# Second stage: projections and softplus sum in front of the skip product, output projection late, gate product between fourth drive and scan

## What is computed

```python
def _mamba(x, in_w, conv_w, conv_b, xproj_w, dt_w, dt_b, A_log, Dvec, out_w):
    xi, z = jnp.split(jnp.einsum('bld,ed->ble', x, in_w), 2, axis=-1)
    xc = silu(causal_conv4(xi) + conv_b)
    dt, Bm, Cm = jnp.split(jnp.einsum('ble,fe->blf', xc, xproj_w), [4, 20], axis=-1)
    dt = softplus(jnp.einsum('blr,er->ble', dt, dt_w) + dt_b)
    # for each of 16 states s, along the sequence:
    #   h = exp(dt * A) * h + dt * B_t * x_t ;  y_t = sum_s h * C_t
    y = (ys + xc * Dvec) * silu(z)
    return jnp.einsum('ble,de->bld', y, out_w)
```

## Time and profile before

| | |
|---|---|
| median of 3 runs | 3953.78 us (3950.43 to 3957.21) |
| the profiled execution | 3949.65 us, its span 3947.8 us |
| PE busy | 3654.2 us, 93% |
| DVE busy | 3749.1 us, 95% |
| ACT busy | 2937.3 us, 74% |
| POOL busy | 3277.5 us, 83% |
| scans (L1601) | 1024, 2297.9 us, 2274 ns each |
| drives by DVE (L1588) | 768, 906.5 us, 1210 ns each |
| reads by POOL (L1537) | 1024, 2398.9 us, 2360 ns each |
| state sums (L1306) | 4096 matmuls, 1921.9 us, 602 ns each |
| read from memory | 1144 MB, 299 GB/s over the span |

### The profile page before, as it was taken

The page is one execution under the profiler, slowest core; times in us unless marked ns, Lnnn a source line. Parts: engine busy times, 40 slices in busy tenths (PEclk is TensorE's granted clock), DMA queues, the critical chain, the costliest instruction groups (busy, mean ns, idle before and its releaser), DMA issues. The chain is left out here.

```text
span 3947.8 us, 34409 instructions
## 1 busy us (share of the span) xinstructions
PE 3654.2 (93%) x8780; PEld 1519.6 (38%) x8780; DVE 3749.1 (95%) x3409; ACT 2937.3 (74%) x4422; POOL 3277.5 (83%) x1542
## 2 busy tenths in 40 slices
PE   7999999899999999999999999999999999999998
PEld 3444444333333333333333333333333333333333
DVE  7778787999999999999999999999999999999998
ACT  3454554787888878888888888878888888878785
POOL 2221222899999999999999999999999999999998
PEclk9999999999999999999999999999999999999999
DMA  4142324888888888898888888888899888988886
GB/s 113 33 130 58 109 74 149 325 344 338 347 348 348 344 345 340 345 350 353 347 342 350 347 347 342 352 347 341 343 353 349 339 346 347 350 340 344 336 348 264
DMA packets 203157, 1181.06 MB, mean 299 GB/s; under 512 B 30960, under 2 KB 31760, under 8 KB 68816
## 3 DMA queue, kind: packets, MB, share of 16 engines
q1 hardware_dynamic: 200128, 1177.64, 77.5%
q10 hardware_dynamic: 2832, 1.23, 0.1%
HBM read 1144.03 MB, written 34.73 MB: 299 GB/s over the span
## 5 line engine op out<-in xcount | busy, mean ns | idle before, releaser
L1537 POOL TENSOR_TENSOR read<-state,bc_all 128x1024 f32<-128x1024 f32 x1024 | 2398.9, 2360 | 117.0 <-DVE state L1601 88.0
L1601 DVE TENSOR_TENSOR_SCAN state<-decays,p_drive 128x1024 f32<-128x1024 f32 x1024 | 2297.9, 2274 | 33.0 <-ACT p_drive L1436 9.8
L1306 PE MATMUL p_y<-read,ident 128*128 128x512 f32 x4096 | 1921.9, 602 | 14.0 <-POOL read L1537 13.9
L1428 ACT ACTIVATE decays<-dt,wa 128x496 f32<-128x496 f32 x2048 | 1337.2, 703 | 121.1 <-DVE state L1601 118.5
L1306 PEld LDWEIGHTS p_y<-read,ident 128*128 128x128 f32 x4096 | 764.9, 191 | 990.6 <-issue 833.2
L1588 DVE TENSOR_TENSOR p_drive<-bc_all,p_dtx 128x1024 f32<-128x1024 f32 x768 | 906.5, 1210 | 0.0
L1554 POOL TENSOR_TENSOR pool_drive<-dtx,bc_all 128x1024 f32<-128x1024 f32 x256 | 602.4, 2353 | 12.2 <-DMA bc_all<-bc_scratch 11.9
L766 POOL TENSOR_TENSOR pad<-map_all,xc 128x512 f32<-128x512 f32 x96 | 138.9, 1476 | 519.1 <-DMA map_all<-map_scratch 498.3
L1436 ACT COPY p_drive<-pool_drive 128x1024 f32<-128x1024 f32 x256 | 260.8, 1019 | 270.8 <-DVE state L1601 270.8
L1302 PE MATMUL p_y<-xconv,d_diag 128*128 128x512 f32 x256 | 144.6, 647 | 202.0 <-DVE gated L1611 202.0
L556 PE MATMUL p_conv<-pad,wm 128*128 128x512 f32 x576 | 267.5, 600 | 1.8 <-issue 1.8
(11 more groups left out here) (162 smaller groups left out, 3214.1 us busy)
## 6 DMA issues: line engine op xcount, KB each, us to landing
bc_all<-bc_scratch SPq DMA_DIRECT2D x1024, 1024.0 KB, 7.3
map_all<-map_scratch SPq DMA_DIRECT2D x48, 512.0 KB, 5.7
norm_rows<-xn SPq DMA_DIRECT2D x32, 280.0 KB, 5.8
norm_in<-norm_rows SPq DMA_DIRECT2D x64, 140.0 KB, 6.6
norm_in<-norm_rows SPq DMA_DIRECT2D x64, 139.8 KB, 7.6
fresh<-in_x SPq DMA_DIRECT2D x32, 256.0 KB, 6.8
x<-in_x SPq DMA_DIRECT2D x32, 256.0 KB, 3.6
mid_x<-x SPq DMA_DIRECT2D x32, 256.0 KB, 6.5
```

The costliest lines, as they stand in the source:

```text
L1306: nc.tensor.matmul(p_y[:], ident[:], read[:, s % DEEP, :], start=False, stop=(s == N - 1)).then_inc(y_added, 1)
L1428: nc.scalar.activation(decays[:, s % DEEP, :].rearrange("p (q t) -> p q t", t=SIDE)[:, :, 1:], dt[b][:, :, 1:], ACT.Exp, scale=wa[m][:, s: ...
L1537: nc.gpsimd.tensor_tensor(read[:, s % DEEP:s % DEEP + 2, :], state[:, s % DEEP:s % DEEP + 2, :], bc_all[s // CHUNK][:, :, 1, :], ALU.mult) ...
L1601: nc.vector.tensor_tensor_scan(state[:, at:at + 2, :].rearrange("p s n -> p (s n)"), decays[:, at:at + 2, :].rearrange("p s n -> p (s n)") ...
```

## The change

It moves work inside the slot of the second stage and adds none. On PE, the softplus sum of u + 1 and both input projections of u + 2 go in front of the skip product at s = 5; B, C and raw dt go from 12 to 10; the output projection of u - 1 goes from 7 to 13. On ACT the copy of dt goes from step 1 to 6, silus from 11 to 8, the copy of B and C and the softplus steps from 13 to 11, the copy out from 8 to 14. On POOL dtx goes from step 5 to 7. On DVE the gate product goes from behind scan 1 to between drive 3 and scan 3. Units 2 and UNITS - 4 keep the output projection early (`AT_OUT_FIRST`), since the next projection needs `cols_in` filled from it. Waits on `left` and `rows_copied` follow the new order. SP's list is not changed.

```diff
-    AT = dict(project_out=7, leave=8, hold_rows=1,
-              project_in=9, project_z=10, silus=11, project_bc=12, project_dt=12, copy_rows=13, soft=13,
-              sum_dt=0, copy_dt=1, dtx=5, copy_dtx=15)
+    AT = dict(hold_rows=1, project_in=5, sum_dt=5, copy_dt=6, dtx=7, silus=8, project_bc=10, copy_rows=11, soft=11,
+              project_out=13, leave=14, copy_dtx=15)
+    AT_OUT_FIRST = dict(AT, project_out=6, leave=7, project_in=8, project_bc=10)
+    OUT_FIRST = (2, UNITS - 4)
...
-        ge(pe, left, u - 2)
+        ge(pe, left, u - 2 if u - 2 in OUT_FIRST else u - 3)
...
         def project_out(u, b, unit, rows_used):
+            ge(pe, left, u)
             pe.wait_ge(rows_copied, rows_used)
...
         def slot(u, b, before, unit, after, later):
+            when = at(u)
             for s in range(N):
+                if s == when["sum_dt"] and after:
+                    sum_dt(pe, u + 1)
+                if s == when["project_in"] and s == LAG and later:
+                    project_conv(pe, u + 2, later)
+                    project_z(pe, u + 2, later)
                 if s == LAG:
                     add_skip(u, b, unit)
...
-                if s == AT["project_out"] and before:
-                    project_out(u - 1, 1 - b, before, u + 2 if after else UNITS)
+                if s == when["project_out"] and before:
+                    rows = u + 2 if u in OUT_FIRST else u + 3
+                    project_out(u - 1, 1 - b, before, min(rows, UNITS))
-                if s == AT["project_in"] and later:
+                if s == when["project_in"] and s > LAG and later:
...
-                if s == AT["sum_dt"] and after:
-                    sum_dt(pe, u + 1)
...
-                if s == AT["leave"] + 1 and u in (2, UNITS - 4):
+                if s == at(u)["leave"] + 1 and u in OUT_FIRST:
...
-                if s == (AT["copy_dt"] if u else 4) and after:
+                if s == AT["copy_dt"] and after:
...
+                scan_pair(u, p + 2)
+                make_drives(u, p + 3)
                 if half == 0 and before:
                     apply_gate(u - 1, 1 - b, before)
-                scan_pair(u, p + 2)
-                make_drives(u, p + 3)
                 scan_pair(u, p + 3)
```

More of the change, by code:

```diff
@@ L1040, in stage2, with at @@
     MOVE_LEAD = 2
-    AT = dict(project_out=7, leave=8, hold_rows=1,
-              project_in=9, project_z=10, silus=11, project_bc=12, project_dt=12, copy_rows=13, soft=13,
-              sum_dt=0, copy_dt=1, dtx=5, copy_dtx=15)
+    AT = dict(hold_rows=1, project_in=5, sum_dt=5, copy_dt=6, dtx=7, silus=8, project_bc=10, copy_rows=11, soft=11,
+              project_out=13, leave=14, copy_dtx=15)
+    AT_OUT_FIRST = dict(AT, project_out=6, leave=7, project_in=8, project_bc=10)
+    OUT_FIRST = (2, UNITS - 4)
+    def at(u):
+        return AT_OUT_FIRST if u in OUT_FIRST else AT
     def sb(name, shape, dt=f32):
@@ L1343, in slot @@
                     project_conv(pe, u + 2, later)
-                if s == AT["project_z"] and later:
                     project_z(pe, u + 2, later)
-                if s == AT["project_bc"] and later:
+                if s == when["project_bc"] and later:
                     project_bc(pe, u + 2, b, later)
-                if s == AT["project_dt"] and later:
                     project_dt(pe, u + 2, b, later)
-                if s == AT["sum_dt"] and after:
-                    sum_dt(pe, u + 1)
         pe.wait_ge(s1["gn_v"], 16)
@@ L1504, in slot @@
                     hold_rows(u - 2, u)
-                if s == AT["leave"] + 1 and u in (2, UNITS - 4):
+                if s == at(u)["leave"] + 1 and u in OUT_FIRST:
                     hold_rows(u - 1, None if u == 2 else u + 1)
-                if s == AT["leave"] and before:
+                if s == at(u)["leave"] and before:
                     if before[0] == ROWS:
```

## The result

The changed kernel takes 4002.35 us (median of 4 runs, 3996.54 to 4005.18) against 3954.91 us for the kernel before on the same chip: a ratio of 1.0121, 95% interval 1.0109 to 1.0134. The change makes the kernel 1.2% slower. The profiled execution's span is 4001.6 us, 53.8 more than before.

What follows compares the result with a forecast made beforehand. VectorE was taken as the bound. From the profiled 3949.65 us: -21.3 (gate's place), -9.8 (old clock falls), +8.8 (two exceptional units), +56.1 (new falls) = 3983 us; the forecast's own range 3960 to 4008, with rival 1 3922 to 4008.

Steps and rivals of the forecast that it cites:

- What bounds the kernel: Second stage: VectorE, busy 990 of 1000 us, sets the clock; one unit takes 25.19 us.
- the gate's 0.17 us: VectorE: the gate product between drive 3 and scan 3 saves 0.17 us a unit, 21.3 us over 125 units.
- Rival 4: VectorE: the drain rule holds and the gate's new place gives nothing, 4004 us; chance 0.03.
- The chain of 18.35 to 18.46 against 18.38: Pair 2's scan to next scan 0: the chain over TensorE and ScalarE equals VectorE's own way within 0.1 us; nothing charged.
- The hole moves and becomes 1.99 and 1.55 us: TensorE's idle wait moves from skip to z: 1.99 us in rows units, 1.55 in cols.
- The falls of the clock: TensorE behind waits before z: 34 drops to 1.2 GHz at 1.65 us each, +56.1 us (bounds 23 and 110).
- the wait's length decides: TensorE: seven clock falls followed some thirty waits of 1.90 us, none those of 1.85; so 1.99 brings more.
- After a fall the next fall is likelier: TensorE: a fall lengthens its next wait by 0.6 us, to 2.6 in rows units and 2.1 in cols.
- The clock rule: TensorE: a skill page warns only of longer idle gaps; by it no wait of this size would cost anything.
- my first rival: TensorE before z: no or few clock falls, so 3927 us, faster; chance 0.25.
- The two exceptional units and the opening: Units 2 and UNITS - 4: 4.4 us each, +8.8, bounds 0 and 6 each; opening and end nothing, +-3.
- the seven old falls: Steady stage of the kernel before: seven clock falls after 1.90 us waits, which the change removes, -9.8 us.

Runs made afterwards that it cites:

- e7: e4 with the gate product back behind scan 1: 3942.39 us, ratio 0.9971 to the kernel before.
- e4: The changed kernel with ScalarE's copy of dt in step 5 instead of 6: 3929.64 us, ratio 0.9939 to the kernel before.
- e6: e2 with the conv of every unit, rows and cols, issued twice to fill the waits: 4005.41 us, ratio 1.0132 to the kernel before.
- e1: The changed kernel with the conv projection of rows units issued twice, filling the wait before z: 3951.37 us, ratio 0.9994 to the kernel before.
- e2: The changed kernel with the gate product back behind scan 1: 4206.76 us, ratio 1.0640 to the kernel before.
- e5: The changed kernel with only the first product of a rows unit's conv issued twice, half e1's filling: 3960.67 us, ratio 1.0022 to the kernel before.
- e3: The kernel before with the gate product alone moved between drive 3 and scan 3: 4630.70 us, ratio 1.1711.
- e10: e4 with the gate product behind scan 1 in units 2 and UNITS - 4 alone: 3917.66 us, ratio 0.9911 to the kernel before.
- e9: e5 with the z product of rows units fed from 128 partitions instead of 64: 3936.61 us, ratio 0.9960 to the kernel before.
- e11: The changed kernel with only the z product of rows units fed from 128 partitions: 3968.60 us, ratio 1.0039 to the kernel before.

## Why the prediction was right, and where it was off

I forecast 3983 us, slower, with 3960 to 4008 as the forecast's own range; 4002 lies near its upper end.

- **What bounds the kernel** and the gate's 0.17 us: right. The undisturbed unit is 25.00 us against 25.02; e7 against e4 gives 0.19 by itself. The page rule of the Trainium skill that I weighed ("VectorE: DVE Perf Modes", "The DRAIN you can't avoid") does not hold for a scan behind its own drive: 0.19 us a unit are there when the scan follows at once and gone with the gate product between. Rival 4, which followed that rule, had 4004 us, nearer to the measured 4002 than my 3983, but for the wrong reason.
- **The chain of 18.35 to 18.46 against 18.38**: right in size. Undisturbed rows units are 25.04 and, the second, 25.21, so the chain is longer than VectorE's way by 0.04 to 0.2 in them, where I had said within 0.1. I charged nothing; over the middle 115 units it costs 8.7 us. e6 measured the chain itself: 25.5 to 25.8 us a unit, against 25.6.
- **The hole moves and becomes 1.99 and 1.55 us**: measured 1.95 in most first rows units, 1.5 to 1.6 in cols, and 2.16 in most second rows units, where I had made no difference. In 13 of the 30 first ones it is only 0.8 to 1.8; where it is 1.2 or less, TensorE had waited longer for reads of GpSimd before. Of the 0.21, ScalarE's step from the drive copy to the copy of dt is 0.08 (2386.08 to 2387.12 is 1.04, against 0.96 in the earlier trace rows); the rest I did not trace.
- **The falls of the clock**: the mechanism was right, shown by e1 (fill the wait, and 51 us are back) and e6 against e2. I took 34 falls in 62 rows units at 1.65. In the middle there are 27, and against the undisturbed unit of their kind they cost 22 times 1.70 and five times 3.35, together 54.0, so 2.0 each. The single fall of 1.65 was right; that one kind costs twice as much I had not seen. In the five the clock was low from z on and for longer, as at 1033.80, where z, skip and six state sums took 10.60 us against the 7.3 of the prediction's terms:

```profile
1033.80 1.80 PE L1257 MATMUL p_b<-norm_in,wi_rows 64*128 64x512 f32 x2 [1.95 <-ACT dt L1404]
1035.52 2.07 PE L1304 MATMUL p_y<-xconv,d_diag 128*128 128x512 f32 x2
1037.39 7.08 PE L1308 MATMUL p_y<-read,ident 128*128 128x512 f32 x12
```

  The product of the two, 56.1 against 54.0, was right partly by luck: fewer falls, and dearer ones. My step "the wait's length decides" failed, in the changed kernel by falls behind 1.61 to 1.69 us and by 23 against 6 in second and first rows units, and again in e5 (falls behind 1.3 us) and e6 (none behind 1.5). What else decides, and why the second rows unit is so much worse, is open. "After a fall the next fall is likelier" did not show: behind a fall come mostly cols units, whose wait stays at 1.59, and after the five large ones the second rows unit waited 2.63 without one. e2 doesn't show it either.
- **The clock rule** (my first rival, by the "HAM oscillation" section of the page "TensorE: Matmul & The Clock Gate" of the Trainium skill): waits of 1.3 to 2.2 us, shorter than its gaps, bring falls; the runs decide against it here. The rival's 3927 us, though, is not what this order takes without falls: less 54.0 us in the middle and 1.7 each in units 4 and 121, the profiled 4003.4 us would be some 3946 (an estimate), as the chain and the ends cost what both had left out. e4's 3930 has another place for the copy of dt.
- **The two exceptional units and the opening**: the step that was most mis-sized. I gave 4.4 us to each and nothing to opening and end. Units 2 and 124 cost 6.0 and 5.9 more than before, at my bound of 6, the units behind them 1.3 each, and units 0 and 1 cost 4.2 and 2.5. In unit 2 TensorE waits 4.29 us for the later gate product and then works at the low clock; the copy of the output ends 11.4 us behind the start of pair 2's scan, where I had 8.8, and VectorE waits 5.9 us for the decays behind it (5.1 in unit 124). In unit 0 it waits 1.4 and 3.0 us for decays, in unit 1 2.6 us for the copy of drive 0; TensorE waits 4.9 and 3.7 us before z in these two, with the clock low at z. Opening and end together cost 23.6 instead of 8.8, two falls of 1.7 (units 4 and 121) among them. These 14.8 us and the chain's 8.7 are more than the 20 us between 3983 and the profiled 4003.4; a little less for the falls (2.1), the gate (0.6), the seven old falls (0.2) and the start (0.6) makes up the rest.

## What to carry to other kernels

Where an engine off the bound is given a new order, look for the place to which its idle time moves, and for what it meets there: here one wait of about 2 us cost more than waits of 1 us and less in another place, since TensorE's clock fell behind it. Work out the chain that ends in the bound's next instruction, and keep some cover in it; here a copy placed one step sooner (e4) gave that cover and turned the sign of the whole change. Move a consumer later on the bound only together with the work that fills its producer's wait (e3, e10).

## What the hardware showed beyond expectation

- Adding 256 matmuls made the kernel 51 us faster (e1), since TensorE kept its 2.4 GHz through the steady stage.
- With 128 instead of 64 rows in the product behind the wait there were fewer falls: none (e9) against nine (e5), and 20 (e11) against 29 (the changed kernel). The wait of the second rows units was also 0.12 us shorter, and e6 has 64 rows behind waits of up to 1.5 us without a fall, so the rows' own share is not settled.
- A fall in nearly every unit makes 27.3 us a unit of the 25.6 that the same order takes without falls (e2, e6).
